# Attention 0 on one Trainium2 core: a masked sum moved to a later batch, and query rows interleaved so that one transfer stacks four heads of four tiles

## Chip, cores and metric

The kernel runs on 1 core of one Trainium2 chip. The metric is the device time of one execution in microseconds (us), as a median of the runs shown. About 0.2% (3 us here) is what such a measurement can tell from no change.

## What is computed

Two layers of a gated model on x, 8 batches of 256 rows by 1024, with a context of the same shape. Only the first attention and a part of the first feed-forward stage matter here:

```
x = x + tanh(g_xattn[0]) * L0_xattn(layernorm(x), ctx, wq, wk, wv, wo, ln_w)
x = x + tanh(g_ffn[0])   * L0_ffn(layernorm(x), W_base, b_base, enc, coefs, mask)
x = x + tanh(g_xattn[1]) * L1_xattn(layernorm(x), ctx, ctx, ...)
x = x + tanh(g_ffn[1])   * L1_ffn(layernorm(x), weight)

# L0_xattn: 32 query heads of 32, 8 key/value heads, each shared by 4 query heads
q = rmsnorm(x) @ wq.T ; k = ctx @ wk.T ; v = ctx @ wv.T
out = softmax(q k.T / sqrt(32)) v ; return out @ wo.T

# L0_ffn: three encoders' coefficients, masked, through an inverse real FFT
w = coefs * mask                      # 3 x 1024 x (32 + 8)
update = sum over e of irfft(enc(x) @ w[e].T)   # linear, so w is summed over e first
```

## The kernel before

The program runs in stages one after the other: keys and values (`c_` names), attention 0 (`a_`), the middle stage with the output projection and the first feed-forward part (`m_`), attention 1 (`b_`), and the quantised last stage (`q_`, `z_`). The change lies in attention 0, the function `attn0_stage`, and in the host's arrangement of the weight `wq`.

**Work and tiles.** The 8 batches run one after the other, two to an iteration of a loop (three iterations; the last two batches, 6 and 7, are written out with `final` set). In a batch the queries are computed transposed, one tile of 128 query rows by 256 positions for each t from 0 to 7, and a tile holds 4 heads of 32 rows. A step n from 0 to 15 is one tile t = n // 2 with one half of the positions. In each step TensorE (PE) does, in order: the transposes of the probabilities of step n (`transposes`, L966), the scores of step n + 2 (`scores`, L956), the values of step n - 1 (`values`, L979 and, every second step, L985), and a piece of the queries of the next batch (`query_step`: four transposes of x at L915 in steps 0 to 3, then matmuls at L931). VectorE (DVE) takes the maximum of the scores (L1063), splits queries into a high and a low part (`split`, L1056 and L1058), and normalises (L1076, L1078). ScalarE (ACT) does the exponentials (L1148) and copies transposed probabilities out of PSUM (L1165). In steps 5, 7, 9 and so on VectorE takes one of the two copies (L1108).

**Precision and stacking.** Queries and keys are split in a high and a low part, and one matmul over 128 contraction rows does all four products of 32 rows each. So for the matmul `q_stack` must hold, for each head, its 32 rows four times one above the other: high, high, low, low. [...] `stack_quad(b, h)` does it for half a batch, four tiles: 16 transfers issued by SyncE (SP), one for each part and head j, 128 KB each:

```
for part, src in enumerate((q_hi, q_hi, q_lo, q_lo)):
    for j in range(JH0):
        sp.dma_start(plain(q_stack)[part * HD0:(part + 1) * HD0, tiles, j, :],
                     plain(src)[j * HD0:(j + 1) * HD0, tiles, :]).then_inc(q_stacked[h], 16)
```

PE waits for `q_stacked[h]` at step 0 and step 8 of the scores (L952); VectorE waits for it before it writes over the first tile of a half.

**SP's order.** Before the loop: keys and values of batch 0, `stack_quad(0, 0)`, then 12 small loads of the coefficients and masks (L807, L809). In a batch: `stack_quad(b, 1)`, x of batch b + 2, keys and values of batch b + 1, the store of the first half of the output, `stack_quad(b + 1, 0)`, the store of the second half.

**The prologue.** Ahead of the loop PE computes all queries of batch 0 and the scores of its steps 0 and 1. VectorE splits 11 of the 12 uses of the query banks, takes the maxima of steps 0 and 1, then waits for the 12 small loads and does the masked sum: a product of 128x960 (L1086) and two sums of 128x320 (L1088, L1090). The 12th split comes after it, as the first thing in the body of batch 0. The result `wsum` is used by PE in batch 7 only (`update_part`, L1006).

Of the kernel before, what the change touches and what calls it, by code (L numbers as in the profile page):

```python
# [17 lines left out]
F32R = mybir.dt.float32r  # L18
# [8 lines left out]
P = 128  # L27
B, S, D = 8, 256, 1024
TT = S // P
KT = D // P  # L30
# [655 lines left out]
def plain(tile):  # L686

    return tile.bitcast(F32)

def attn0_stage(nc, sh, c, scratch, wq, rows, norm):
# [14 lines left out]
    Q_USES = XFILLS + KT  # L706
    QUAD = KT // 2
    BANK0_DVE = set(range(XFILLS + 1, UNITS, 2))
    QUAD_DMAS = JH0 * 4

    COPY_STEP = {f + 1: f for f in range(XFILLS)}
    for t in range(KT - 1):
# [1 line left out]
    with ExitStack() as es:  # L714
# [8 lines left out]
        xT_lo = sb("xT_lo", [P, KT, S], F32R)  # L723
        q_hi = sb("q_hi", [P, KT, S], F32R)
        q_lo = sb("q_lo", [P, KT, S], F32R)
        q_stack = sb("q_stack", [P, KT, JH0, S], F32R)
        k_stack = sb("k_stack", [P, 2, NKV0, S], F32R)
        v0 = sb("v0", [P, 2, TT, KV0])
        prob = sb("prob", [P, 2, JH0, S])
# [40 lines left out]
        def _(sp):  # L770
# [16 lines left out]
            def stack_quad(b, h):  # L787

                sp.wait_ge(psQ_lo, Q_USES * b + XFILLS + QUAD * (h + 1) + 1)
                tiles = slice(QUAD * h, QUAD * (h + 1))  # L790
                for part, src in enumerate((q_hi, q_hi, q_lo, q_lo)):
                    for j in range(JH0):
                        sp.dma_start(plain(q_stack)[part * HD0:(part + 1) * HD0, tiles, j, :],
                                     plain(src)[j * HD0:(j + 1) * HD0, tiles, :]).then_inc(q_stacked[h], 16)

            def store_quad(b, h):

# [103 lines left out]
        def _(pe):  # L901
# [46 lines left out]
            def scores(b, i, u, n):  # L948

                t, qb = n // TT, n % TT  # L950
                if n % (UNITS // 2) == 0:
                    pe.wait_ge(q_stacked[t // QUAD], 16 * QUAD_DMAS * (b + 1) + 1)  # L952
                if n == 0:
                    pe.wait_ge(kv_loaded[u], 16 * 5 * (i + 1))
                for j in range(JH0):
                    last = nc.tensor.matmul(psS[:, 2 * (n % 2) + j // 2, (j % 2) * S:(j % 2 + 1) * S],  # L956
                                            q_stack[:, t, j, qb * P:(qb + 1) * P],
                                            k_stack[:, u, (t // REP0) * JH0 + j, :], start=True, stop=True)
                last.then_inc(scores_full, 1)

# [77 lines left out]
        @block.vector  # L1038
        def _(dve):
            dve.sem_inc(psT_copied[0], 1)  # L1040
            dve.sem_inc(psQ_lo, 1)
            dve.sem_inc(o_ready, 1)
            def split(b, use, prologue=False):

                bank = psS[:, use % 4, :] if prologue else psQ[:, :]
                dve.wait_ge(psQ_full, Q_USES * b + use + 1)
                if use < XFILLS:
                    cols = slice(2 * use, 2 * use + 2)
                    hi, lo, src = xT_hi[:, cols, :], xT_lo[:, cols, :], bank.rearrange("p (k n) -> p k n", k=2)
                    high = plain(xT_hi)[:, cols, :]  # L1050
                else:
                    t = use - XFILLS
                    if t % QUAD == 0:
                        dve.wait_ge(q_stacked[t // QUAD], 16 * QUAD_DMAS * b + 1)
                    hi, lo, src, high = q_hi[:, t, :], q_lo[:, t, :], bank[:, 0:S], plain(q_hi)[:, t, :]
                nc.vector.tensor_copy(hi, src).then_inc(psQ_hi, 1)  # L1056
                dve.wait_ge(psQ_hi, Q_USES * b + use + 1)
                nc.vector.tensor_tensor(lo, src, high, ALU.subtract).then_inc(psQ_lo, 1)  # L1058

            def maximum(b, n):  # L1060
                dve.wait_ge(scores_full, UNITS * b + n + 1)
                bank = 2 * (n % 2)
                nc.vector.tensor_reduce(negmax[:, n % 2, :], psS[:, bank:bank + 2, :].rearrange("p a (j k) -> p (a j) k", k=S),  # L1063
                                        AX_X, ALU.max, negate=True).then_inc(max_ready, 1)

            def low_of_wo(n):
                dve.wait_ge(rows.wo_high, n + 1)
                nc.vector.tensor_tensor(wq.lo[:, n, :], rows.blocks[n % 4], plain(wq.hi)[:, n, :], ALU.subtract
                                        ).then_inc(rows.wo_split, 1)

            def normalise_o(b, t):

                if t % QUAD == 0:
                    dve.wait_ge(o_stored[t // QUAD], 16 * b + 1)
                dve.wait_ge(psO_full, KT * b + t + 1)
                nc.vector.tensor_copy(recipT[:, :], psO[:, 1, :]).then_inc(recipT_ready, 1)  # L1076
                dve.wait_ge(recipT_ready, KT * b + t + 1)
                nc.vector.tensor_tensor(oT[:, t, :], psO[:, 0, :], recipT[:, :], ALU.mult).then_inc(o_ready, 1)  # L1078

            for use in range(Q_USES - 1):
                split(0, use, True)
            maximum(0, 0)
            maximum(0, 1)
            dve.wait_ge(coefs_loaded, 16 * 4 * NE)
            nc.vector.tensor_tensor(coefs[:, :, :, :], coefs[:, :, :, :], masks[:, :, :, :], ALU.mult).then_inc(masked_done, 1)  # L1086
            dve.wait_ge(masked_done, 1)
            nc.vector.tensor_tensor(wsum[:, :, :], coefs[:, 0, :, :], coefs[:, 1, :, :], ALU.add).then_inc(masked_done, 1)  # L1088
            dve.wait_ge(masked_done, 2)
            nc.vector.tensor_tensor(wsum[:, :, :], wsum[:, :, :], coefs[:, 2, :, :], ALU.add).then_inc(summed, 1)  # L1090

            def copy_update(quarter):
                dve.wait_ge(update_full, quarter + 1)
                nc.vector.tensor_scalar(update[:, quarter * QUARTER:(quarter + 1) * QUARTER], psQ[0:RR, 0:QUARTER], 0.5, None, ALU.mult
                                        ).then_inc(update_copied, 1)

            def body(i, final):
                for u in range(2):
                    b = 2 * i + u
                    more = not (final and u == 1)  # L1100
                    for n in range(UNITS):
                        if n == 0:
                            split(b, Q_USES - 1)
                        elif n in COPY_STEP and more:
                            split(b + 1, COPY_STEP[n])
                        if n in BANK0_DVE:
                            dve.wait_ge(psT_full[0], UNITS * b + n + 1)
                            nc.vector.tensor_copy(probT[:, n % 2, 0, :, :],  # L1108
                                                  psT[:, 0, :].rearrange("p (j q) -> p j q", j=JH0)).then_inc(psT_copied[0], 1)
                        if n % 2:  # L1110
                            t = n // 2
                            dve.wait_ge(exp_done, UNITS * b + n + 1)
                            nc.vector.reciprocal(recip_head[:, t % 2], sums[:, t % 2]).then_inc(head_ready, 1)  # L1113
                        if n + 2 < UNITS:
                            maximum(b, n + 2)
                        elif more:
                            maximum(b + 1, n + 2 - UNITS)
                        if n and n % 2 == 0:
                            normalise_o(b, n // 2 - 1)
                            if not more:  # L1120
                                low_of_wo(n // 2 - 1)

                        if n == 6 and not final:
                            dve.wait_ge(x_loaded[u], 16 * i + 16)
                            norm.stats_of(x[:, u], 0)
                        if n == 9 and not final:
                            norm.moments_of(dve, b + 2, x[:, u], last_tile_only=True)
                        if n == 12 and not final:
                            norm.normalise(dve, b + 2, x[:, u], x[:, u], norm.STEPS_RMS)
                        if n > UPDATE_STEP and (n - UPDATE_STEP) % 3 == 0 and not more:  # L1130
                            copy_update((n - UPDATE_STEP) // 3 - 1)
                    normalise_o(b, KT - 1)
                    if not more:
                        copy_update(3)
                        low_of_wo(KT - 1)

            with dve.Fori(0, PAIRS - 1) as i:
                body(i, False)
            body(PAIRS - 1, True)
# [1295 lines left out]
def layouts(inputs):  # L2435
# [2 lines left out]
    lay, a = {}, {short: np.asarray(inputs[name]) for short, name in _NAMES.items()}  # L2438
    lay["ctxT"] = np.stack([halves(transposed_tiles(a["ctx"][b])) for b in range(B)])
    lay["wkT"], lay["wvT"] = halves(transposed_tiles(a["wk"])), halves(transposed_tiles(a["wv"]))  # L2440
    by_tile = a["wq"].reshape(HALF0, JH0, REP0, HD0, D).transpose(0, 2, 1, 3, 4).reshape(D, D)
    lay["wqT"] = transposed_tiles(by_tile).transpose(1, 0, 2)
    lay["ln_col"] = a["ln_w"].reshape(KT, P).T
    lay["projs"] = np.concatenate([a["proj_k"], a["proj_v"]], axis=1).reshape(KT, P, 2 * NK1).transpose(1, 0, 2)
# [31 lines left out]
```

## Time and profile before

| | |
|---|---|
| median of 3 runs | 1495.08 us (1495.05 to 1495.64) |
| the profiled execution | 1496.8 us, span 1495.1 us |
| PE busy | 1377.2 us (92%), 10782 matmuls |
| DVE busy | 971.4 us (65%) |
| ACT busy | 745.9 us (50%) |
| POOL busy | 426.3 us (29%) |
| transfers | 127910 packets, 174.93 MB, of which 96919 packets under 2 KB |
| mean granted TensorE clock | 0.966 |

Times in the trace are counted from the start of the span. Attention 0 with its prologue runs from about 150 to 692 us. "Idle before" an instruction is time in which its engine did nothing, and the name behind the arrow is what ended it; "issue" means that the profile shows no engine's work as the releaser. PEld is the weight load of a matmul and overlaps PE. A busy PE is not a PE at its peak: its records overlap, so ends of matmuls are modelled.

### The profile page before, as it was taken

To read this page: it belongs to the slowest core of one execution; us is meant where nothing else is said; L and a number is where in the kernel's file an instruction comes from. 1 tells how busy PE (TensorE), PEld (TensorE's weight loads), DVE (VectorE), ACT (ScalarE), POOL (GpSimd) and SP (SyncE) were. 2 spreads that over 40 slices of the span, in tenths; PEclk is the share of its full clock that TensorE was granted. 3 is DMA by queue.
4 is the path that set the end of the run, shared out by engine and by line. 5 is a ranking of instruction groups with operands and counts; after the bars stand their busy time and mean duration, and the time that the engine had idled before them with its cause. 6 is when DMAs were issued, how large, how long until landed. Compare 5 with 4: busy or idle time off the path is not lost. (4 is left out here: it accounts for less than half of the span.)

```text
span 1495.1 us, 28528 instructions
## 1 busy us (share of the span) xinstructions
PE 1377.2 (92%) x10782; PEld 1120.8 (75%) x10782; DVE 971.4 (65%) x1564; ACT 745.9 (50%) x1881; POOL 426.3 (29%) x473
## 2 busy tenths in 40 slices
PE   6998789989989999987999999999779999999388
PEld 6998778979889898865888888888556666666144
DVE  4363277777767767565232256578567999998597
ACT  4231167766757767763111110113157777777396
POOL 0010001101010110010110232232358888887324
PEclk9999889999999999999999999999889999999789
DMA  6742454553544536464445452112332222221023
GB/s 224 244 155 85 90 126 117 139 146 77 145 110 120 147 96 167 125 197 150 166 167 197 157 210 99 56 36 84 113 81 65 62 64 64 63 64 43 1 85 141
DMA packets 127910, 174.93 MB, mean 117 GB/s; under 512 B 27799, under 2 KB 96919, under 8 KB 127792
## 3 DMA queue, kind: packets, MB, share of 16 engines
q1 hardware_dynamic: 127792, 173.26, 39.9%
q8 instruction: 86, 1.41, 0.4%
q14 instruction: 32, 0.26, 0.1%
HBM read 86.94 MB, written 35.29 MB: 82 GB/s over the span
## 5 line engine op out<-in xcount | busy, mean ns | idle before, releaser
L1148 ACT ACTIVATE a_prob<-a_psS,a_negmax 128x256 f32<-128x256 f32 x512 | 236.7, 483 | 158.6 <-DVE a_negmax L1063 158.4
L1063 DVE TENSOR_REDUCE a_negmax<-a_psS 128x4 f32<-128x1024 f32 x128 | 154.1, 1204 | 68.1 <-PE a_psS L956 66.5
L881 POOL COPY a_recip<-a_recip_head 128x256 f32<-128x256 f32 x64 | 25.6, 400 | 526.5 <-DVE a_recip_head L1113 526.5
L931 PE MATMUL a_psQ<-a_xT_hi,wide 128*128 128x256 f32 x912 | 170.9, 288 | 0.4
L1375 PE MATMUL m_psY<-wide,m_a_hi 128*128 128x512 f32 x512 | 159.3, 393 | 6.8 <-DVE m_a_lo L1423 6.8
L1375 PE MATMUL m_psY<-w_ffn,m_a_hi 128*128 128x512 f32 x512 | 158.3, 390 | 0.0
L966 PE MATMUL a_psT<-ident,a_prob 128*128 128x128 f32 x1024 | 138.0, 279 | 14.1 <-issue 6.1
L931 PEld LDWEIGHTS a_psQ<-a_xT_hi,wide 128*128 128x128 f32 x912 | 138.7, 189 | 9.1 <-issue 5.9
L1165 ACT COPY a_probT<-a_psT 128x512 f32<-128x512 f32 x208 | 115.8, 609 | 36.7 <-PE a_psT L966 35.6
L966 PEld LDWEIGHTS a_psT<-ident,a_prob 128*128 128x128 f32 x1024 | 116.7, 143 | 23.0 <-issue 12.7
L931 PE MATMUL a_psQ<-a_xT_lo,wide 128*128 128x256 f32 x456 | 127.5, 280 | 0.0
L1375 PEld LDWEIGHTS m_psY<-wide,m_a_hi 128*128 128x128 f32 x512 | 96.8, 189 | 27.5 <-DVE m_a_lo L1423 7.0
L1375 PEld LDWEIGHTS m_psY<-w_ffn,m_a_hi 128*128 128x128 f32 x512 | 95.6, 188 | 19.5
L1148 ACT ACTIVATION_READ_ACCUMULATOR a_prob<-a_psS,a_negmax 128x1 f32 x512 | 109.4, 214 | 0.0
L2115 ACT ACTIVATE b_prob<-b_prob 128x1024 f32<-128x1024 f32 x64 | 67.9, 1061 | 79.1 <-DVE b_prob L1989 79.1
L1375 PE MATMUL m_psY<-wide,m_a_lo 128*128 128x512 f32 x256 | 100.2, 392 | 0.0
L1375 PE MATMUL m_psY<-w_ffn,m_a_lo 128*128 128x512 f32 x256 | 99.7, 389 | 0.0
L956 PE MATMUL a_psS<-a_k_stack,a_q_stack 128*128 128x256 f32 x512 | 94.1, 307 | 2.9 <-issue 2.9
L1983 DVE TENSOR_REDUCE b_maxes<-b_psS 128x16 f32<-128x1024 f32 x64 | 77.9, 1217 | 27.1 <-PE b_psS L1891 26.0
L1901 PEld LDWEIGHTS b_psT<-ident,b_prob 128*128 128x128 f32 x512 | 60.2, 142 | 35.2 <-issue 32.9
L931 PEld LDWEIGHTS a_psQ<-a_xT_lo,wide 128*128 128x128 f32 x456 | 85.7, 188 | 0.0
L1820 POOL TENSOR_TENSOR b_halves<-b_prob 128x512 f32<-128x512 f32 x64 | 82.5, 1290 | 6.6 <-ACT b_prob L2115 6.0
(233 smaller groups left out, 3013.9 us busy)
## 6 DMA issues: line engine op xcount, KB each, us to landing
a_q_stack<-a_q_hi SPq DMA_DIRECT2D x128, 128.0 KB, 2.6
a_q_stack<-a_q_lo SPq DMA_DIRECT2D x128, 128.0 KB, 2.6
c_raw<-lay_ctxT SPq DMA_DIRECT2D x16, 512.0 KB, 4.8
rows<-in_x SPq DMA_DIRECT2D x8, 1024.0 KB, 6.4
scratch_o<-a_oT SPq DMA_DIRECT2D x16, 512.0 KB, 3.0
m_x<-in_x SPq DMA_DIRECT2D x8, 1024.0 KB, 5.9
scratch_x<-m_x SPq DMA_DIRECT2D x8, 1024.0 KB, 5.1
b_q_stack<-b_q_hi SPq DMA_DIRECT2D x64, 128.0 KB, 2.3
```

What stands on the lines that cost most here:

```text
L881: nc.gpsimd.tensor_copy(recip[:, t % 2], recip_head[:, t % 2].unsqueeze(3).broadcast_to([P, TT, JH0, HD0])).then_inc(recip_ready, 1)
L931: last = nc.tensor.matmul(bank[:, 0:S], w[:, kt, t * P:(t + 1) * P], a[:, kt, :], start=(kt == 0 and w is wq.hi and a is xT_hi), stop=(kt ...
L956: last = nc.tensor.matmul(psS[:, 2 * (n % 2) + j // 2, (j % 2) * S:(j % 2 + 1) * S], q_stack[:, t, j, qb * P:(qb + 1) * P], k_stack[:, u, ...
L966: last = nc.tensor.transpose(psT[:, kt, j * P:(j + 1) * P], prob[:, n % 2, j, kt * P:(kt + 1) * P], ident[:, :])
L1063: nc.vector.tensor_reduce(negmax[:, n % 2, :], psS[:, bank:bank + 2, :].rearrange("p a (j k) -> p (a j) k", k=S), AX_X, ALU.max, negate=Tr ...
L1148: last = nc.scalar.activation(prob[:, n % 2, j, :], psS[:, 2 * (n % 2) + j // 2, (j % 2) * S:(j % 2 + 1) * S], ACT.Exp, bias=negmax[:, n % ...
L1165: nc.scalar.copy(probT[:, n % 2, kt, :, :], psT[:, kt, :].rearrange("p (j q) -> p j q", j=JH0)).then_inc(psT_copied[kt], 1)
L1375: last = nc.tensor.matmul(psY[:, 2 * t + h, :], a[:, u, kt, rows_t], m[:, kt, cols], start=(kt == 0 and a is a_hi and m is w.hi), stop=(kt ...
L1820: nc.gpsimd.tensor_tensor(halves[:, n % 2], unit[:, :, 0:NK1 // 2], unit[:, :, NK1 // 2:NK1], ALU.add).then_inc(halves_ready, 1)
L1901: last = nc.tensor.transpose(psT[:, t, j * P:(j + 1) * P], prob[:, n % 2, (4 * t + j) * P:(4 * t + j + 1) * P], ident[:, :])
L1983: nc.vector.tensor_reduce(maxes[:, n % 2, :], psS[:, n % 2, :].rearrange("p (h k) -> p h k", h=NH1), AX_X, ALU.max).then_inc(max_ready, 1)
L2115: nc.scalar.activation(prob[:, n % 2, :], prob[:, n % 2, :], ACT.Exp).then_inc(exp_done, 1)
```

## The change

Four edits. `QUAD_DMAS` falls from 16 to 4. `q_stack` has its dimensions head and tile exchanged, and one transfer takes all 128 partitions of a part's source, four tiles in a row (4 KB for each partition), and writes 32 partitions with four heads each. For this the host puts the rows of `wq` in another order, so that in a tile the row c of head j is partition 4 c + j and not 32 j + c. The masked sum becomes a function and is called in batch 6 (`final`, u = 0) at step 6, behind `normalise_o`.

```diff
-    QUAD_DMAS = JH0 * 4
+    QUAD_DMAS = 4
...
-        q_stack = sb("q_stack", [P, KT, JH0, S], F32R)
+        q_stack = sb("q_stack", [P, JH0, KT, S], F32R)
...
                 for part, src in enumerate((q_hi, q_hi, q_lo, q_lo)):
-                    for j in range(JH0):
-                        sp.dma_start(plain(q_stack)[part * HD0:(part + 1) * HD0, tiles, j, :],
-                                     plain(src)[j * HD0:(j + 1) * HD0, tiles, :]).then_inc(q_stacked[h], 16)
+                    sp.dma_start(plain(q_stack)[part * HD0:(part + 1) * HD0, :, tiles, :],
+                                 plain(src)[:, tiles, :]).then_inc(q_stacked[h], 16)
...
-                                            q_stack[:, t, j, qb * P:(qb + 1) * P],
+                                            q_stack[:, j, t, qb * P:(qb + 1) * P],
...
             maximum(0, 0)
             maximum(0, 1)
-            dve.wait_ge(coefs_loaded, 16 * 4 * NE)
-            nc.vector.tensor_tensor(coefs[:, :, :, :], coefs[:, :, :, :], masks[:, :, :, :], ALU.mult).then_inc(masked_done, 1)
...
+            def masked_sum():
+                dve.wait_ge(coefs_loaded, 16 * 4 * NE)
...
+                        if n == 6 and final and u == 0:
+                            masked_sum()
                         if n == 6 and not final:
...
-    by_tile = a["wq"].reshape(HALF0, JH0, REP0, HD0, D).transpose(0, 2, 1, 3, 4).reshape(D, D)
+    by_tile = a["wq"].reshape(HALF0, JH0, REP0, HD0, D).transpose(0, 2, 3, 1, 4).reshape(D, D)
```

The instructions in order, at the places where it matters. VectorE at the end of the prologue, before the change (the branch is the entry of the loop, the CAST after it the 12th split):

```order
L1063 TENSOR_REDUCE a_negmax<-a_psS 128x4 x2
L1086 TENSOR_TENSOR a_coefs<-a_coefs,a_masks 128x960
L1088 TENSOR_TENSOR a_wsum<-a_coefs 128x320
L1090 TENSOR_TENSOR a_wsum<-a_wsum,a_coefs 128x320
L1137 UNCONDITIONAL_BRANCH
L1137 ISA
L1056 CAST a_q_hi<-a_psQ 128x256
L1058 TENSOR_TENSOR a_q_lo<-a_psQ,a_q_hi 128x256
```

and with the change (its line numbers are one lower here, two higher for the loop):

```order
L1062 TENSOR_REDUCE a_negmax<-a_psS 128x4 x2
L1139 UNCONDITIONAL_BRANCH
L1139 ISA
L1055 CAST a_q_hi<-a_psQ 128x256
L1057 TENSOR_TENSOR a_q_lo<-a_psQ,a_q_hi 128x256
L1060 ISA
L1062 TENSOR_REDUCE a_negmax<-a_psS 128x4
```

The 12th split now follows the two maxima directly. VectorE in batch 6, steps 6 and 7, with the change:

```order
L1062 TENSOR_REDUCE a_negmax<-a_psS 128x4 x2
L1075 COPY a_recipT<-a_psO 128x256
L1077 TENSOR_TENSOR a_oT<-a_psO,a_recipT 128x256
L1086 TENSOR_TENSOR a_coefs<-a_coefs,a_masks 128x960
L1088 TENSOR_TENSOR a_wsum<-a_coefs 128x320
L1090 TENSOR_TENSOR a_wsum<-a_wsum,a_coefs 128x320
L1055 CAST a_q_hi<-a_psQ 128x256
L1057 TENSOR_TENSOR a_q_lo<-a_psQ,a_q_hi 128x256
L1108 COPY a_probT<-a_psT 128x512
L1113 RECIPROCAL a_recip_head<-a_sums 128x8
```

The three instructions stand ahead of a split of batch 7's second query tile, where before the split followed the normalisation. SP in the prologue, before:

```order
L793 DMA a_q_stack<-a_q_hi 32x4x256 x8
L793 DMA a_q_stack<-a_q_lo 32x4x256 x8
L807 DMA a_coefs<-in_coefs 128x8x32
L809 DMA a_masks<-in_mask 128x8x32
```

and with the change:

```order
L792 DMA a_q_stack<-a_q_hi 32x4x1024 x2
L792 DMA a_q_stack<-a_q_lo 32x4x1024 x2
L806 DMA a_coefs<-in_coefs 128x8x32
L808 DMA a_masks<-in_mask 128x8x32
```

Sixteen transfers of rows of 1 KB became four of rows of 4 KB, and the same holds at each of the 16 stackings.

## Rows read from the trace of the kernel before

**Rows 1.** The page, part 1: busy time of the engines, share of the span, instructions.

```profile
PE 1377.2 (92%) x10782; PEld 1120.8 (75%) x10782; DVE 971.4 (65%) x1564; ACT 745.9 (50%) x1881; POOL 426.3 (29%) x473
```

**Rows 2.** Waits by engine: us in total, times, longest; attention 0 and its prologue.

```profile
PE a_psQ L915 <- DVE a_q_lo L1058: 6.8, 5, 5.1
PE a_psS L956 <- issue: 2.9, 1, 2.9
DVE a_coefs L1086 <- DMA a_masks<-in_mask: 5.7, 1, 5.7
```

**Rows 3.** Timeline of SP's queue, first stacking: start, duration, engine, line, what.

```profile
166.76 5.87 SPq L793 DMA_DIRECT2D a_q_stack<-a_q_hi  x8
172.68 5.14 SPq L793 DMA_DIRECT2D a_q_stack<-a_q_lo  x8
```

**Rows 4.** Timeline of the prologue's end; in brackets idle time before and its releaser.

```profile
179.64 1.18 PE L956 MATMUL a_psS<-a_k_stack,a_q_stack 128*128 128x256 f32 x8 [2.94 <-issue]
180.39 2.35 DVE L1063 TENSOR_REDUCE a_negmax<-a_psS 128x4 f32<-128x1024 f32 x2 [5.49 <-PE a_psS L956]
...
181.65 0.47 ACT L1148 ACTIVATE a_prob<-a_psS,a_negmax 128x256 f32<-128x256 f32 x1 [43.33 <-DVE a_negmax L1063]
...
183.63 1.97 PE L966 MATMUL a_psT<-ident,a_prob 128*128 128x128 f32 x8 [2.81 <-ACT a_prob L1148]
...
185.25 1.11 ACT L1165 COPY a_probT<-a_psT 128x512 f32<-128x512 f32 x2
185.25 1.20 PE L956 MATMUL a_psS<-a_k_stack,a_q_stack 128*128 128x256 f32 x4
...
188.46 1.16 DVE L1086 TENSOR_TENSOR a_coefs<-a_coefs,a_masks 128x960 f32<-128x960 f32 x1 [5.71 <-DMA a_masks<-in_mask]
...
191.04 0.42 DVE L1058 TENSOR_TENSOR a_q_lo<-a_psQ,a_q_hi 128x256 fp32r<-128x256 f32 x1
191.38 1.22 DVE L1063 TENSOR_REDUCE a_negmax<-a_psS 128x4 f32<-128x1024 f32 x1
...
191.52 1.11 PE L915 MATMUL a_psQ<-ident,rows 128*128 128x128 f32 x4 [5.06 <-DVE a_q_lo L1058]
...
195.70 0.66 PE L915 MATMUL a_psQ<-ident,rows 128*128 128x128 f32 x4
196.20 1.04 PE L966 MATMUL a_psT<-ident,a_prob 128*128 128x128 f32 x8
...
196.49 0.47 ACT L1148 ACTIVATE a_prob<-a_psS,a_negmax 128x256 f32<-128x256 f32 x1 [0.97 <-DVE a_negmax L1063]
```

**Rows 5.** Windows of 1 us: stretch, us, PE busy, granted clock, DMA share, GB/s.

```profile
172.00:173.00 1.00, 1.00 (x11) 1.00 0.85 204
176.00:177.00 1.00, 0.70 (x7) 1.00 0.88 209
...
206.00:207.00 1.00, 1.00 (x11) 1.00 1.00 406
```

**Rows 6.** DMA issues: what, queue, count, KB each, median us to landing.

```profile
a_q_stack<-a_q_hi SPq DMA_DIRECT2D x128, 128.0 KB, 2.6
```

**Rows 7.** Timelines of batch 0: last issues of the next batch's stacking, its first scores.

```profile
234.35 5.17 SPq L793 DMA_DIRECT2D a_q_stack<-a_q_lo  x8
...
248.10 0.72 PE L956 MATMUL a_psS<-a_k_stack,a_q_stack 128*128 128x256 f32 x4
```

**Rows 8.** Timelines of VectorE and PE in batch 6, steps 6 and 7.

```profile
587.65 0.42 DVE L1078 TENSOR_TENSOR a_oT<-a_psO,a_recipT 128x256 f32<-128x256 f32 x1
...
588.88 0.42 DVE L1058 TENSOR_TENSOR a_q_lo<-a_psQ,a_q_hi 128x256 fp32r<-128x256 f32 x1
...
590.24 0.50 PE L931 MATMUL a_psQ<-a_xT_hi,wide 128*128 128x256 f32 x2
```

**Rows 9.** Windows around three stops of PE, columns as in Rows 5.

```profile
180.00:185.00 5.00, 2.19 (x14) 0.65 0.89 82
...
310.00:317.00 7.00, 4.06 (x56) 1.00 0.29 93
438.00:446.00 8.00, 4.80 (x30) 0.79 0.59 165
```

More of the change, by code:

```diff
@@ L1084, in _ @@
             maximum(0, 1)
-            dve.wait_ge(coefs_loaded, 16 * 4 * NE)
-            nc.vector.tensor_tensor(coefs[:, :, :, :], coefs[:, :, :, :], masks[:, :, :, :], ALU.mult).then_inc(masked_done, 1)
[L1087 to L1090, printed above, removed]
+            def masked_sum():
+                dve.wait_ge(coefs_loaded, 16 * 4 * NE)
+                nc.vector.tensor_tensor(coefs[:, :, :, :], coefs[:, :, :, :], masks[:, :, :, :], ALU.mult).then_inc(masked_done, 1)
+                dve.wait_ge(masked_done, 1)
+                nc.vector.tensor_tensor(wsum[:, :, :], coefs[:, 0, :, :], coefs[:, 1, :, :], ALU.add).then_inc(masked_done, 1)
+                dve.wait_ge(masked_done, 2)
+                nc.vector.tensor_tensor(wsum[:, :, :], wsum[:, :, :], coefs[:, 2, :, :], ALU.add).then_inc(summed, 1)
             def copy_update(quarter):
```

## The prediction, made before the changed kernel was run

> **What bounds the kernel.** I read the page first, then the waits of attention 0, then the timeline of its prologue, and last the places where the moved work lands. PE is busy 92% of the span [rows 1], so what matters is PE's idle time and whatever delays PE. In the list of waits two of PE's entries touch the change: 2.9 us ahead of the scores, which the profile puts down to "issue", and 6.8 us in five waits for a split, of which one alone is 5.1 [rows 2]. Both long ones lie in the prologue.
>
> *First stop.* PE works through the 8th query until 176.7 (in the window from 176 it is busy 0.70) [rows 5] and starts the scores at 179.64 after 2.94 us [rows 4]. No engine's work ends that wait, so it is a transfer: SP issues 16 stacking transfers from 166.76 to 177.82 [rows 3], 11.06 / 16 = 0.69 us each, and one takes 2.6 us to land [rows 6]. The last, issued at about 177.2, lands at about 179.6. The stack is the last to come.
>
> *Second stop.* After the transposes of step 0 and the scores of step 2 PE ends at 185.25 + 1.20 = 186.45 and stands 5.06 us until 191.52, for a split of VectorE (done 191.04 + 0.42) [rows 4]. The split stood in line behind the masked sum, and that behind 5.71 us of waiting for the last mask; the sum starts at 188.46 [rows 4]. ACT is held too: the maximum of step 2 comes at 191.38 only.
>
> **Stacking by 4 transfers.** The bytes are the same, 16 x 128 KB = 2.10 MB. With rows of 1 KB the 16 DMA engines are 0.85 busy and move 204 GB/s; a transfer with rows of 4 KB from memory moves 406 GB/s at 1.00 [rows 5]. That row is no copy within SBUF, so both ends stay open: at best 2.10 MB / 406 GB/s = 5.2 us, at worst the rate per busy engine stays (204 / 0.85 = 240 GB/s, 8.7 us) or nothing at all is gained (10.3 us at 204). Data now starts about 1.3 us after the first issue (10.3 us of data must end by 179.6 less some 1 us of completion; 166.8 + 1.3 + 10.3 = 178.4). So the stack lands at 166.8 + 1.3 + 5.2 + 1.2 = 174.5, at 178.0, or at 179.6. PE is free at 176.7. The term is 2.94 us, 1.6 us, or 0; more than 2.94 is excluded, since PE has its queries to do until then. I take 2.94: the row of 4 KB rows is nearest in shape. SP's four issues at 0.69 us are 2.8 us and don't bind; even at three times that price they would end at 175.
>
> The Trainium skill ("DMA: Bandwidth & Descriptors", section "Why small descriptors are slow (HBM only)") speaks against this: copies from SBUF to SBUF don't suffer from short descriptors. No row here shows such a copy with long rows. By that rule the rate would not rise, which is the rival below.
>
> At the other 15 stackings nobody waits for the stack. Example: the stacking for batch 1 is issued until 234.35 + 5.17 = 239.5, landed by 242.1, and its first scores run at 248.10 without idle time [rows 7]: 6 us of room. Landing some 5 us earlier there gives 0. SP is free 8 us earlier, so x, keys and values of later batches come earlier; nobody waits for them either: 0. In the prologue the 12 small loads move forward too and share the DMA engines with nothing that is awaited, since their reader is 400 us away; if they ran into the next stacking, that has over 10 us of room.
>
> **Prologue without the masked sum.** What is late next has to be walked through. I move the chain by 2.94 us and drop the wait; all times of this walk come from [rows 4] unless another group is named. Scores of steps 0 and 1 run 176.70 to 177.88, both maxima end at 182.74 - 2.94 = 179.80, the 12th split follows at once and is done at 180.7. The exponentials start at 178.71; the transposes of step 0 at 180.69.
> - At full clock (a score group 0.72 us as in [rows 7], four transposes of x 0.66, eight of probabilities about 0.8 until the next) the scores of step 2 end at 182.2, their maximum at 183.5. ACT meanwhile ends the exponentials of step 1 at 182.4 and two copies at 183.5, does those of step 2 until 185.4, two more copies until 186.5, and starts the exponentials of step 3 at 186.5. Before it was 196.49. From there on ACT and PE both run without long stops, as before. Gain 10.0.
> - At half clock (1.20, 1.11 and 1.6 us, as at 183 to 192) the scores of step 2 end at 183.5, the maximum at 184.85, the scores of step 3 at 187.4, the maximum at 188.6: exponentials of step 3 at 188.6. Gain 7.9.
>
> Which clock? Before, it fell to 1.2 GHz soon after the two short stops (0.65 in the stretch 180 to 185). PE now stops once, 177.88 to 180.69, 2.8 us. The same length of stop left the clock at 2.4 GHz at 313 and took it down at 440 [rows 9]. So either is possible, or half of each, and I take the middle, **9.0 us** for both terms together, of which 2.94 hang on the stack.
>
> **The masked sum in batch 6.** The three instructions take 191.04 - 0.42 - 0.03 - 188.46 = 2.1 us, with their own waits (start to the next CAST, at 190.6) [rows 4]. In batch 6, VectorE ends the normalisation at 588.07 and its next split at 589.30; PE takes that split's bank at 590.24, without a wait [rows 8]. With the sum ahead, the split runs 590.25 to 591.15, so PE stands about **0.9 us**. The bounds are 0 (if PE is late there itself) and 2.1. The maximum of step 9 slips by 1.8 us, and PE wants its exponentials only in the step after the next, some 3.8 us on: 0. The loads were there long before: no wait. In the other batches the layer's statistics stand at this place; batch 6 has none.
>
> **Elsewhere.** The scores' matmuls read as many contiguous columns as before: 0. The stops of PE at the loop's end (313, 440) are PE's own and stay. But all later work moves by some 8 us, and whether a short stop takes the clock down seems a matter of when it comes. A fall costs up to 1.7 us (0.79 mean clock over 8 us is 0.42 x 8 = 3.4 us at half clock, and half of that is lost) [rows 9]. I set 0 with 2 us each way.
>
> **Sum.** 9.0 - 0.9 = 8.1 us. The profiled execution took 1496.8 us, 1.7 more than its span and than the median of 1495.08; against it the sum gives 1488.7, and the runs 1495.1 - 8.1 = **1487.0 us**.
>
> **Rivals.**
> - *The rate doesn't rise.* The stack lands at 179.6 as before, the first stop stays and only the second goes. For: the DMA engines are already 0.85 busy. Against: 406 GB/s with long rows [rows 5]. By the rule of the Trainium skill cited above this would be the outcome. The chain then keeps its old times until 186.45, at half clock: maximum of step 2 until 187.8, scores of step 3 until 190.3, exponentials of step 3 at 191.5, 4.9 us earlier, less 0.9: 1491.1 us. If only the per-engine rate stays (178.0) it is about 1488.5. Chance 0.13.
> - *Four transfers land on few DMA engines.* A transfer writes 32 partitions from 128; if it were served by a quarter of the engines, 2.10 MB at some 100 GB/s would be 21 us, with issue and landing 23. Against the room: the stacking for batch 1 starts some 16 x 0.69 = 11 us before 239.5, at 228.5, and is needed at 248.1 [rows 7], 20 us later. PE would stand 3 us or more at each of 15 places, 45 us, and 12 in the prologue: about 1540 us. It decides from 20 us for one stacking. Against: today's transfers also write 32 partitions, and use the engines at 0.85. Chance 0.03.
> - *The gain is lost again*, by two or three more falls of the clock and a larger price in batch 6 (2.1): about 1493 us. Against: no transfer at a fixed time ends attention 0. Chance 0.05.
>
> **Numbers.** The forecast as it stands has 0.79. About 0.2% (3 us) is what a measurement of this kernel can tell from no change. Faster: the forecast and most of the first rival, 0.90; within 0.2%: the third and a rest of the first, 0.07; slower: 0.03. The range goes from 10.0 - 0.9 + 2 = 11.1 less, 1484.0, to the first rival, 1491.1.
>
> **What would show it.** In the changed profile: stacking issues of x4 in under 4 us; PE's scores at 176.7 (right) or 179.6 (first rival); no wait of 5 us at L915; exponentials of step 3 between 186.5 and 188.6; a PE wait near 1 us for the split in batch 6; GB/s during a stacking near 400 or near 200. I am wrong if the scores or the split find another wait in their place, or if PE stands for a stack in mid-stage.

## The result and the profile after

The changed kernel takes **1573.11 us** (median of 4 runs, 1569.83 to 1576.58) against 1495.07 us of the kernel before (4 runs, 1494.56 to 1495.64): ratio 1.0522, interval 1.0491 to 1.0554. It is 78.0 us slower. The forecast was 8.1 us faster; the time lies far outside the range of 1484.0 to 1491.1.

The page of the changed kernel, its span, part 1, the DMA queue of part 3, the group of the scores in part 5, and the issues of part 6 (KB each, median us to landing):

```profile
span 1574.6 us, 28328 instructions
PE 1402.8 (89%) x10774; PEld 1140.3 (72%) x10782; DVE 972.4 (62%) x1564; ACT 746.5 (47%) x1881; POOL 426.7 (27%) x473
q1 hardware_dynamic: 100144, 173.24, 46.8%
L955 PE MATMUL a_psS<-a_k_stack,a_q_stack 128*128 128x256 f32 x512 | 97.6, 316 | 41.1 <-DMA a_q_stack<-a_q_lo 31.4
a_q_stack<-a_q_hi SPq DMA_DIRECT2D x32, 512.0 KB, 10.3
a_q_stack<-a_q_lo SPq DMA_DIRECT2D x32, 512.0 KB, 16.4
```

DVE, ACT and POOL are busy as long as before, to 1 us [rows 1]; only PE differs, 1402.8 us against 1377.2. The scores now stand idle 41.1 us, 31.4 of it for the stack, where the stack had cost one stop of 2.9 us [rows 2]. A transfer of the stack lands after 10.3 or 16.4 us, where one of a quarter of its size took 2.6 [rows 6]. The DMA engines carry the same bytes and are busy longer (46.8% of a longer span; the page of before has 39.9%).

The prologue of the changed kernel: timelines of SP and PE, and a window of 2 us during the first stacking (columns as in rows 5):

```profile
167.78 2.14 SPq L792 DMA_DIRECT2D a_q_stack<-a_q_hi  x2
169.96 1.37 SPq L792 DMA_DIRECT2D a_q_stack<-a_q_lo  x2
...
175.76 10.99 SPq L806 DMA_DIRECT2D a_coefs<-in_coefs  x1
```
```profile
187.43 2.04 PE L955 MATMUL a_psS<-a_k_stack,a_q_stack 128*128 128x256 f32 x8 [9.72 <-issue]
...
194.52 1.06 PE L914 MATMUL a_psQ<-ident,rows 128*128 128x128 f32 x4
```
```profile
172.00:174.00 2.00, 2.00 (x20) 1.00 1.05 123
```

SP issues the stack in 3.6 us instead of 11 [rows 3], as forecast. But the data moves at 123 GB/s instead of 204 [rows 5], and the DMA engines are full (share 1.05). All 16 take part: the trace has 16 completions of each of the four transfers, spread over at most 1.1 us, and the four are complete one after the other, at 174.96, 179.26, 183.55 and 187.34. The scores start at 187.43 instead of 179.64 [rows 4]; 2.10 MB at 123 GB/s are 17 us, and from the first issue to the scores it is 19.7. SP itself is caught behind it: the issue of one small load takes 10.99 us. The second stop (5.06 us ahead of L915 in rows 4, L914 here) is gone, as forecast.

In the loop the slow stack costs much more than the waits that bear its name. Batch 0 and the start of batch 1, timelines of SP, PE and VectorE:

```profile
237.71 2.42 SPq L792 DMA_DIRECT2D a_q_stack<-a_q_hi  x2
240.17 1.37 SPq L792 DMA_DIRECT2D a_q_stack<-a_q_lo  x2
```
```profile
257.45 1.02 PE L955 MATMUL a_psS<-a_k_stack,a_q_stack 128*128 128x256 f32 x4 [3.02 <-DMA a_q_stack<-a_q_lo]
...
297.16 0.50 PE L930 MATMUL a_psQ<-a_xT_hi,wide 128*128 128x256 f32 x2 [1.91 <-DVE a_q_lo L1057]
```
```profile
295.04 1.28 DVE L590 BATCH_NORM_STATS2 norm_stats<-rows 128x6 f32<-128x512 f32 x2 [2.17 <-DMA rows<-in_x]
```

The stack that is issued from 237.71 releases PE at 257.45, after a stop of 3.02 us. The next load of x queues behind a stacking and is late (VectorE waits 2.17 us for it), so the split is late, and PE stops 1.91 us more. And the granted clock falls after stops. The window of PE at the stop of 3.02 us has 0.71, part of it at 1.2 GHz:

```profile
256.00:260.00 4.00, 2.54 (x23) 0.71 0.01 1
```

The same work in both kernels, by the windows of PE, all of attention 0 and one batch: of before,

```profile
160.00:693.00 533.00, 496.27 (x5380) 0.97 0.51 129
222.77:283.88 61.11, 60.08 (x675) 1.00 0.50 127
```

and of the changed kernel:

```profile
160.00:773.50 613.50, 523.88 (x5389) 0.93 0.67 112
232.59:305.35 72.76, 64.11 (x675) 0.95 0.67 106
```

This accounts for the result: the stage is 80.5 us longer, of which 52.9 are idle time of PE (613.50 - 523.88 = 89.6 against 36.7) and 27.6 are longer matmuls, the same ones at a lower granted clock (0.93 in the mean against 0.97). This one batch costs 11.65 us more, 7.6 idle and 4.0 slower. The windows of one batch start with the store of the first half of batch 0's output. There the changed kernel is only 9.8 us late (232.59 against 222.77); some 70 us come after that. Nothing outside the stage adds to it.

### The profile page after: what moved, and what is told of

Its sections match the earlier page's. It is cut to its first block and busy times, and to the rows that moved or that the text cites. A ratio compares the mean times of both kernels' runs of the same rounds, so it can differ in the third digit from the quotient of the medians.

```text
span 1574.6 us, 28328 instructions
## 1 busy us (share of the span) xinstructions
PE 1402.8 (89%) x10774; PEld 1140.3 (72%) x10782; DVE 972.4 (62%) x1564; ACT 746.5 (47%) x1881; POOL 426.7 (27%) x473
## 3 DMA queue, kind: packets, MB, share of 16 engines
q1 hardware_dynamic: 100144, 173.24, 46.8%
## 5 line engine op out<-in xcount | busy, mean ns | idle before, releaser
L930 PE MATMUL a_psQ<-a_xT_hi,wide 128*128 128x256 f32 x912 | 179.7, 298 | 5.9 <-DVE a_q_lo L1057 5.6
L965 PE MATMUL a_psT<-ident,a_prob 128*128 128x128 f32 x1024 | 141.8, 283 | 24.8 <-issue 14.4
L930 PEld LDWEIGHTS a_psQ<-a_xT_hi,wide 128*128 128x128 f32 x912 | 146.2, 199 | 15.3 <-DVE a_q_lo L1057 9.2
L965 PEld LDWEIGHTS a_psT<-ident,a_prob 128*128 128x128 f32 x1024 | 120.0, 146 | 34.8 <-issue 21.4
L955 PE MATMUL a_psS<-a_k_stack,a_q_stack 128*128 128x256 f32 x512 | 97.6, 316 | 41.1 <-DMA a_q_stack<-a_q_lo 31.4
L930 PE MATMUL a_psQ<-a_xT_lo,wide 128*128 128x256 f32 x456 | 131.5, 288 | 0.0
L955 PEld LDWEIGHTS a_psS<-a_k_stack,a_q_stack 128*128 128x128 f32 x512 | 73.7, 203 | 44.1 <-issue 29.7
L978 PE MATMUL a_psO<-a_probT,a_v 128*32 128x128 f32 x2048 | 87.6, 289 | 3.8 <-issue 3.8
L930 PEld LDWEIGHTS a_psQ<-a_xT_lo,wide 128*128 128x128 f32 x456 | 90.2, 198 | 0.0
## 6 DMA issues: line engine op xcount, KB each, us to landing
a_q_stack<-a_q_hi SPq DMA_DIRECT2D x32, 512.0 KB, 10.3
a_q_stack<-a_q_lo SPq DMA_DIRECT2D x32, 512.0 KB, 16.4
```

Of the source, the lines that this page charges most:

```text
L930: last = nc.tensor.matmul(bank[:, 0:S], w[:, kt, t * P:(t + 1) * P], a[:, kt, :], start=(kt == 0 and w is wq.hi and a is xT_hi), stop=(kt ...
L965: last = nc.tensor.transpose(psT[:, kt, j * P:(j + 1) * P], prob[:, n % 2, j, kt * P:(kt + 1) * P], ident[:, :])
L978: nc.tensor.matmul(psO[j * HD0:(j + 1) * HD0, 0, qb * P:(qb + 1) * P], v0[:, u, kt, head * HD0:(head + 1) * HD0], probT[:, n % 2, kt, j, : ...
```

## The experiments

Three theories of the slow rate. *P* (*M* in the first expectations): it comes from the mapping, that is, from which partitions the transfer reads and writes at one time. *R*: it comes from the rows of 4 KB. *N*: it comes from there being few, large transfers. Ahead of them stands the question whether the stacking is the cause at all, or the masked sum. Experiment 1 starts from the kernel before, all others from the changed one. Every kernel computes all of the reference.

**1. The masked sum alone.** The kernel before, with the second half of the change only:

```diff
-            dve.wait_ge(coefs_loaded, 16 * 4 * NE)
...
+            def masked_sum():
+                dve.wait_ge(coefs_loaded, 16 * 4 * NE)
...
+                        if n == 6 and final and u == 0:
+                            masked_sum()
```

> Only the masked sum is moved to batch 6; the stacking is that of the kernel before. Theory A (all of the loss is the stacking's): PE's 5.06 us stop in the prologue goes, its 2.94 us stop ahead of the first scores stays, PE pays about 0.9 us in batch 6, so some 4 us faster than before, about 1491 us. Theory B (the moved sum costs in batch 6 or later, or upsets the clock): 1495 us or more.

Measured 1489.79 us (10 runs) against 1494.65 (25 runs), ratio 0.9969 (0.9955 to 0.9983). Its timelines of PE, prologue and batch 6:

```profile
178.62 1.18 PE L956 MATMUL a_psS<-a_k_stack,a_q_stack 128*128 128x256 f32 x8 [2.94 <-issue]
...
584.16 0.50 PE L931 MATMUL a_psQ<-a_xT_hi,wide 128*128 128x256 f32 x2 [0.75 <-DVE a_q_lo L1058]
```

The sum is worth 4.9 us by the medians: the second stop goes, the first stays at its 2.94 us, and batch 6 costs 0.75.

**2. The stacking alone**, with the masked sum left in the prologue:

```diff
-            def masked_sum():
-                dve.wait_ge(coefs_loaded, 16 * 4 * NE)
...
+            dve.wait_ge(coefs_loaded, 16 * 4 * NE)
...
-                        if n == 6 and final and u == 0:
-                            masked_sum()
```

> Only the stacking is changed (4 transfers with rows of 4 KB from 128 interleaved partitions); the masked sum stays in the prologue. Theory A: nearly all of the 78 us are here, 1573 us and up to 8 us more, since in the prologue the sum now waits for masks that land after 194 us. Theory B: clearly below 1573 us.

Measured 1568.88 us (2 runs), ratio 1.0497 (1.045 to 1.0545). The loss belongs to the stacking: it alone costs 74 us. That it came out some 4 us below the changed kernel and not up to 8 above it is a miss; two runs 7 us apart don't carry more than that.

**3. Rows of 4 KB, 32 partitions to 32.** The interleaving of `wq` undone, the new layout of the stack kept: 16 transfers as before, each with one row of 4 KB for each partition instead of four of 1 KB.

```diff
-    QUAD_DMAS = 4
+    QUAD_DMAS = JH0 * 4
...
-                    sp.dma_start(plain(q_stack)[part * HD0:(part + 1) * HD0, :, tiles, :],
-                                 plain(src)[:, tiles, :]).then_inc(q_stacked[h], 16)
+                    for j in range(JH0):
+                        sp.dma_start(plain(q_stack)[part * HD0:(part + 1) * HD0, j, tiles, :],
+                                     plain(src)[j * HD0:(j + 1) * HD0, tiles, :]).then_inc(q_stacked[h], 16)
...
-    by_tile = a["wq"].reshape(HALF0, JH0, REP0, HD0, D).transpose(0, 2, 3, 1, 4).reshape(D, D)
+    by_tile = a["wq"].reshape(HALF0, JH0, REP0, HD0, D).transpose(0, 2, 1, 3, 4).reshape(D, D)
```

> The masked sum in batch 6; the weights' rows in the order of before, 16 transfers of 128 KB for a stacking, each from 32 partitions to 32, but with the new order of the tile, so rows of 4 KB in place of 1 KB. Theory R (long rows are what makes a copy within SBUF slow): about 118 GB/s while stacking, first scores at about 187 us, 1560 to 1580 us. Theory M (the mapping of 128 interleaved partitions into 32 is what is slow) and theory N (few large transfers are): 200 GB/s or more, first scores by 179.6 us, about 1488 to 1491 us.

Measured 1490.01 us (8 runs), ratio 0.9979 (0.9964 to 0.9994). Window during the stacking:

```profile
172.00:174.00 2.00, 2.00 (x20) 1.00 0.89 205
```

205 GB/s with rows of 4 KB, 204 with rows of 1 KB [rows 5], and R falls: rows of 4 KB alone don't give 123. Both run close to SP's own pace, 16 issues in some 10.5 to 11 us, so the rates don't show what either could do beyond it. The time of a packet (in both kernels a packet is one row) does: in the traces' packet records of 172 to 174 us one of 4 KB takes 296 ns here (median), and one of 1 KB 71 ns in the kernel before, for each byte the same to 5%.

**4. Rows of 1 KB, 128 partitions to 32 neighbours.** The interleaving kept, one transfer for each tile:

```diff
-                    sp.dma_start(plain(q_stack)[part * HD0:(part + 1) * HD0, :, tiles, :],
-                                 plain(src)[:, tiles, :]).then_inc(q_stacked[h], 16)
+                    for t in range(QUAD * h, QUAD * (h + 1)):
+                        sp.dma_start(plain(q_stack)[part * HD0:(part + 1) * HD0, :, t, :],
+                                     plain(src)[:, t, :]).then_inc(q_stacked[h], 16)
```

> The masked sum in batch 6; interleaved weights' rows as in the change, but 16 transfers of 128 KB, one for each part and tile, each from 128 partitions to 32 with rows of 1 KB. Theory R (long rows are slow): 200 GB/s, about 1491 us. Theory M (the mapping is slow): about 118 GB/s with rows of 1 KB too, 1560 to 1580 us. Theory N (few large transfers are slow): 200 GB/s, about 1491 us; R and N are told apart by the run with 16 transfers and rows of 4 KB.

Measured 1493.43 us (8 runs), ratio 0.9989 (0.9972 to 1.0005). Window and timeline of PE:

```profile
172.00:174.00 2.00, 2.00 (x20) 1.00 1.13 164
```
```profile
181.42 2.04 PE L956 MATMUL a_psS<-a_k_stack,a_q_stack 128*128 128x256 f32 x8 [5.52 <-issue]
```

No theory in its plain form gives 164 GB/s. But the engines are full (1.13) at a rate below 204, so the shape from 128 partitions to 32 is slow with short rows too, only less so than with long ones.
**5. Destination partitions with a step of 4.** The changed kernel with one edit in the loads of `k_stack` and one in those of `q_stack`. The stack's row r of a part stands in partition 4 r + part; keys and queries are permuted alike, so the scores stay the same sums.

```diff
-                    sp.dma_start(plain(k_stack)[part * HD0:(part + 1) * HD0, u, :, :],
+                    sp.dma_start(plain(k_stack)[part:P:4, u, :, :],
...
-                    sp.dma_start(plain(q_stack)[part * HD0:(part + 1) * HD0, :, tiles, :],
+                    sp.dma_start(plain(q_stack)[part:P:4, :, tiles, :],
```

> The change, with one difference: part p of the stack goes to partitions p, 4 + p, 8 + p and so on up to 124 + p, not to the 32 partitions from 32 p on; the keys are stacked in the same order. Still 4 transfers of 512 KB from 128 interleaved partitions with rows of 4 KB. 
Measured 1486.59 us (4 runs) against 1495.60 (13 runs), ratio 0.9935 (0.9916 to 0.9953). Window, issues, and timeline of PE and ACT:

```profile
172.00:174.00 2.00, 2.00 (x20) 1.00 1.02 340
```
```profile
a_q_stack<-a_q_hi SPq DMA_DIRECT2D x32, 512.0 KB, 4.1
a_q_stack<-a_q_lo SPq DMA_DIRECT2D x32, 512.0 KB, 5.4
```
```profile
177.64 1.12 PE L955 MATMUL a_psS<-a_k_stack,a_q_stack 128*128 128x256 f32 x8
...
187.86 0.47 ACT L1150 ACTIVATE a_prob<-a_psS,a_negmax 128x256 f32<-128x256 f32 x1 [0.37 <-DVE a_negmax L1062]
```

Same four transfers, bytes, source and length of row; only the partitions written are others (no load of the keys runs in this window), and the rate goes from 123 to 340 GB/s. N falls with it, since these are four large transfers too. Both stops of the prologue are gone, and the time is the one that was forecast for the change.

**6. A step of 2.** The same, with each part in every second partition of one half of the 128, so that it spans 64 of them:

```diff
-                    sp.dma_start(plain(q_stack)[part:P:4, :, tiles, :],
+                    sp.dma_start(plain(q_stack)[64 * (part // 2) + part % 2:64 * (part // 2 + 1):2, :, tiles, :],
```

(and `k_stack` alike)

> As the run with the step of 4 partitions, but with a step of 2: parts 0 and 1 interleaved in partitions 0 to 63, parts 2 and 3 in 64 to 127. Theory P: each half of a transfer still meets in half of the groups, 4 engines to a group of partitions, so about 118 GB/s, 1560 to 1580 us. A simpler theory C (the rate goes with the number of partitions that a destination spans, 64 in place of 32, or any spreading helps): 200 GB/s or more, below 1500 us.

Measured 1574.18 us (2 runs), ratio 1.0522 (1.049 to 1.0554). Window:

```profile
172.00:174.00 2.00, 2.00 (x20) 1.00 1.08 123
```

Spread over 64 partitions instead of 32 neighbours, and nothing gained. Scattering the rows doesn't help as such; the step that reaches all of the 128 does.

**7. The source spread, the destination neighbours.** 16 transfers of 32 partitions, rows of 4 KB, reading every fourth partition:

```diff
+                    for j in range(JH0):
+                        sp.dma_start(plain(q_stack)[part * HD0:(part + 1) * HD0, j, tiles, :],
+                                     plain(src)[j:P:JH0, tiles, :]).then_inc(q_stacked[h], 16)
```

> The interleaved source of the change, but one transfer per head and part: 16 transfers of 128 KB, each from 32 partitions at a step of 4 (all over the 128) to 32 neighbouring ones, rows of 4 KB. Theory P: each engine has two neighbouring rows of the destination and all groups are written at once, 200 GB/s (the pace of the 16 issues), first scores at 178.5 to 179.6 us, about 1490 us. Theory X (engines that read in one place and write in another are slow): about 118 GB/s, 1560 us or more.

Measured 1493.43 us (8 runs), ratio 0.9984 (0.9969 to 0.9999). Window:

```profile
176.00:178.00 2.00, 2.00 (x19) 1.00 1.03 166
```

A miss for both theories of the expectation, which wanted 200 or 118. Against experiment 3 only the source changed, and the rate fell from 205 to 166 with full engines. So the rate depends on the source too. This stays open.

**8. Rows of 2 KB, 128 to 32 neighbours.** Eight transfers of two tiles each:

```diff
+                    for t in range(QUAD * h, QUAD * (h + 1), 2):
+                        sp.dma_start(plain(q_stack)[part * HD0:(part + 1) * HD0, :, t:t + 2, :],
+                                     plain(src)[:, t:t + 2, :]).then_inc(q_stacked[h], 16)
```

> The mapping of the change, 8 transfers of 256 KB with rows of 2 KB (two tiles each). Theory P: the two halves of a transfer last half as long, so that engines of one half run beside engines of the other more often: between the 160 GB/s of rows of 1 KB and the 118 of rows of 4 KB, about 135 GB/s. A theory of one fixed rate for the mapping: 118 or 160.

Measured 1526.60 us (one run, so without an interval; before 1495.60). Window and wait of PE:

```profile
172.00:174.00 2.00, 2.00 (x20) 1.00 1.07 135
```
```profile
PE a_psS L956 <- DMA a_q_stack<-a_q_lo: 10.2, 8, 1.8
```

The rate is the one that P named. The number of transfers changes with the length of the row here (4, 8 and 16 in the changed kernel, this one and experiment 4), and no run keeps the two apart.

This also gives the dose. At 164 GB/s (experiment 4) the kernel is 3.6 us slower than with the masked sum alone, and 2.6 of these are the longer stop of the prologue (5.52 against 2.94), so the loop loses little; at 135 it is 31 us slower than before, at 123 it is 78. 2.10 MB take 12.8, 15.5 and 17 us, and with start and completion some 2.5 us more, so somewhere between the first two the room ends.

**9. A better version.** Experiment 5 run once more, and with it a version in which the masked sum stands at step 5 instead of 6:

```diff
-                        if n == 6 and final and u == 0:
+                        if n == 5 and final and u == 0:
```

> The run with the step of 4 partitions once more, for the comparison with the next one on the same chip: 1485 to 1488 us, the masked sum at step 6 of batch 6 and PE's wait of 0.75 us behind it.

> The step of 4 partitions, and the masked sum of batch 6 one step earlier, behind the maximum of step 5, where VectorE stands idle for 2.16 us before its next maximum and the sum takes 2.1. Theory A (the sum costs only what it delays): PE's wait of 0.75 us is gone, 0.7 us less, which the median can hardly show. Theory B (PE has another wait in its place): the same time with a wait of PE elsewhere in batch 6.

Measured, for experiment 5 once more, 1486.77 us (6 runs), ratio 0.9943 (0.9928 to 0.9959), and for the sum at step 5 1485.08 (6 runs), ratio 0.9933 (0.9912 to 0.9954), against 1494.87 (11 runs). Waits of PE from 540 to 620, at step 6 and then at step 5:

```profile
PE a_psQ L930 <- DVE a_q_lo L1057: 0.8, 1, 0.8
PE a_psQ L914 <- DVE a_q_lo L1057: 0.5, 1, 0.5
```
```profile
PE a_psQ L914 <- DVE a_q_lo L1057: 0.5, 1, 0.5
PE a_psT L965 <- ACT a_probT L1167: 0.4, 1, 0.4
```

The 0.8 us of batch 6 are gone. That the time is shorter by as much can't be told from these medians, since the intervals overlap. Either version beats both kernels, the kernel before by 8 to 10 us and the changed one, which was measured apart from them, by some 86 to 88.

## Why the prediction was wrong

**The step that failed: "at worst ... nothing at all is gained (10.3 us at 204)".** The term for the stack was bounded from below by the rate of today's transfers, and no reason was given why the new shape could not be slower. It was: 2.10 MB took some 17 us at 123 GB/s (in the prologue the scores waited 9.72 us instead of 0). The same bound stood behind "at the other 15 stackings nobody waits for the stack", a term of 0, and there most of the time went: some 70 of the 80.5 us of the stage. The value taken, 406 GB/s, came from a row in which memory is the source. Length of row was the wrong likeness: experiment 3 has rows of 4 KB at 205 GB/s. (So the rule that the prediction cited from the Trainium skill, that short descriptors don't slow copies within SBUF, agrees with the runs, but it says nothing of the other thing that the change altered.) What decided here is which partitions are written (experiments 5 and 6: 340 and 123 with source, bytes, rows and number of transfers alike), and no row of before had a transfer from 128 partitions to 32.

The Trainium skill ("SBUF — State Buffer", section "Door 1: The DMA port swizzle (why `[64,N]` ≈ `[32,N]`)") says that four neighbouring partitions share a port, that the partition 32 further on shares it too, and that a transfer's rate goes with the number of ports it reaches: 32 neighbours, or 64, reach 8 of 16. By its formula every fourth of 128 partitions reaches all. The runs agree in the order (123 for 64 partitions with a step of 2, the same as for 32 neighbours; 340 for a step of 4). They differ in size: by its figure of about 27.2 GB/s for a port, 8 ports would be some 218 GB/s, an estimate that allows the 205 of experiment 3 but doesn't explain 123. The missing factor of nearly two would follow from the section "The descriptor swizzle" of the Trainium skill's page "DMA: Bandwidth & Descriptors", if it may be turned round. It says that in a transfer to 128 partitions each DMA engine writes the partitions 4k to 4k+3 and those 32 further on. Here the 128 partitions are the source, for which that section gives nothing; suppose that the engines share them in the same way. With the interleaving an engine's first four then fill one destination partition and its last four the one 8 further on, so that all engines together write 16 of the 32 at a time, 4 ports, an estimated 109 GB/s. That is how P was put after experiment 4. Experiments 6 and 8 came out as it said, 5 nearly so (340 GB/s where it wanted 350 or more), and 7 did not.

The traces don't show which engine carries which row, but their packet records bear on it. In these windows some 14 to 17 packets are under way, and what changes is how long one of 4 KB takes (medians of 172 to 174 us, of experiment 7 176 to 178): 160 ns in experiment 5, 296 in experiment 3, 394 in experiment 7, 588 in the changed kernel and 622 in experiment 6. So the changed kernel isn't held up by idle engines but by packets that take 3.7 times as long. That looks like one, two and four engines sharing one way into SBUF, which is what P says, and 394 fits none of these. The sharing itself is inferred and not shown.

**"6 us of room."** The row at 248.10 [rows 7] belongs to a later step of the batch. The first scores that need the stack are the second line here, in the timelines of SP and PE of the kernel before:

```profile
227.91 6.40 SPq L793 DMA_DIRECT2D a_q_stack<-a_q_hi  x8
...
244.39 0.72 PE L956 MATMUL a_psS<-a_k_stack,a_q_stack 128*128 128x256 f32 x4
```

The issues start at 227.91, so a stacking has 16.5 us from its first issue, not 20. The changed kernel shows the same: issued from 237.71, wanted at 257.45 - 3.02 = 254.43, 16.7 us later. With the forecast rates this made no difference; with a slow one the loss begins at 16.5 us and not at "20 us for one stacking".

**The rival of the few engines** named the rate (100 GB/s against 123) and the sign, but with the wrong mechanism, so that the rate is right by luck. It thought of a quarter of the engines at work, and was dismissed since "today's transfers also write 32 partitions, and use the engines at 0.85". In the changed kernel all 16 engines complete their part of every transfer of the first stacking, at a share of 1.05, and yet are slow: a busy share says that an engine has something under way, not that it moves it at full rate (1.02 at 340 GB/s in experiment 5). A chance of 0.03 was too low for a shape that no row showed. Its price, 45 + 12 us, was too small as well. The waits at the scores in the loop are close to what it said or below (31.4 us in 12 stops). What it left out is what queues behind the stack (x, and through it the splits), and the clock after the stops, which alone is 27.6 us.

**What held.** SP's four issues take 3.6 us and don't bind. The second stop went with the masked sum. The masked sum costs 0.73 us in batch 6 of the changed kernel and 0.75 in experiment 1 (forecast 0.9, bounds 0 and 2.1). The walk through the prologue is borne out by experiment 5: its first split comes 1.1 us later than before, and its exponentials of step 3 at 187.86, which is 186.8 in the time of before, inside 186.5 to 188.6. Its gain by the medians is 9.0 us, and 8.1 when it was run again, where 8.1 was the sum. The rival "the rate doesn't rise" is experiment 3 (1490.01; forecast 1491.1). So the account of the stops was right, and one price was taken from the wrong row.

**What stays open.** The source's part in the rate (experiment 7). And stops of PE behind "issue" at the transposes of the loop: of the changed kernel, and then of experiment 5,

```profile
PE a_psT L965 <- issue: 14.4, 5, 4.5
PE a_psT L965 <- issue: 5.8, 2, 3.0
```

where the kernel before has 6.1 us in 2. So some 8 us of the loss lie there and hang on the slow stack as well. The trace names no releaser. But in each of the two stops of before and of experiment 5 a transfer of the instruction queue (16 KB, q8 in part 3 of the page) starts 0.1 to 0.6 us after PE stops, lasts 1.0 to 1.2, and PE goes on 1.6 to 1.7 us after its end. In the longest stop of the changed kernel, 209.58 to 214.12, two such transfers run from 210.80 to 213.09. That PE waits for its instructions there, and that these too are late behind the stack, fits, but no run tested it.

## What to carry to other kernels

Before merging transfers into SBUF, write down for each which partitions it reads and writes, and compare with a transfer of the same pair in the trace; if there is none, the bound below is not today's rate, however alike the bytes and rows. Where the order of the contracted rows is free, as in this stack, let a small part write every fourth partition of all 128 and not 32 neighbours: it is one slice for each operand (the keys must be permuted alike), and worth a factor of 2.8 in the rate here. And measure the room of a transfer from its first issue to the very first instruction that needs it; what queues behind a late one can cost as much as the wait itself.

## What the runs showed of the hardware

- The same four transfers from 128 to 32 partitions ran at 123 GB/s to 32 neighbours, 123 to every second of 64, and 340 to every fourth of 128, with the engines' share at 1.05, 1.08 and 1.02.
- To 32 neighbours from all 128, the rate rises as the rows get shorter and the transfers more: 123 GB/s with 4 of 4 KB rows, 135 with 8 of 2 KB, 164 with 16 of 1 KB. From 32 to 32 the length didn't matter (205 at 4 KB, 204 at 1 KB, near SP's pace; 296 and 71 ns for a packet).
- Writing 32 neighbours in 16 transfers with rows of 4 KB, it was 205 GB/s where 32 neighbours were read and 166 where every fourth of 128 was.
- At the slow rate the engines are not idle: some 17 packets are under way, and one of 4 KB takes 588 ns (changed kernel) instead of 160 (experiment 5).
- Issuing isn't free when the transfers drain slowly: SP stood 10.99 us in the issue of one small load behind four large transfers at 123 GB/s; behind the same four at 340 (experiment 5) none took over 1.90.
